# Four-layer attention kernel on one core: layer 0's slots placed anew, split weight products and split context made once, layer 2 in two blocks

## What is computed

```
# layer 0: grouped attention, 32 heads, 8 key heads, 16 wide, norm behind it
q = x@Wq+bq;  k = ctx@Wk+bk;  v = ctx@Wv+bv
x = norm(softmax(q k^T/4 + mask) v @ Wo + bo + x) * gamma + beta
# layer 1: token mixing with a state, then channel mixing
xa = norm(x);  sx = shift(xa) - xa;  t = tanh((xa + sx*maa_x) @ maa_w1)
xw, xk, xv, xr, xg = xa + sx*(maa_j + (t @ maa_w2)_j);  w = exp(-exp(...))
out_l = r_l (faaaa*k_l v_l + s);  s = k_l v_l + w_l s         # 100 steps, 32 heads
x = x + (headnorm(out) * silu(xg@Wg.T)) @ Wo.T
xc = norm(x);  x = x + sigmoid(xr2@fWr.T) * (relu(xk2@fWk.T)^2 @ fWv.T)
# layer 2: one head, 512 wide
x = x + alpha * (softmax((x w_q^T)(ctx w_k^T)^T / sqrt(512)) (ctx w_v^T)) w_o^T
# layer 3: two cross attentions (16 heads, 128 wide, one more key and value), then an MLP (2048)
x = x + attention(norm(x), ctx)   # twice;   x = x + gelu(norm(x)@w_fc1+b)@w_fc2+b
```

## Time and profile before

| | before |
|---|---|
| median of 3 runs | 2740.22 us (2735.76 to 2745.87) |
| the profiled execution's own time | 2739.51 us |
| its span, first to last instruction | 2737.7 us |
| mean granted clock of TensorE | 0.95 |
| PE busy | 2478.0 us (91%) |
| PE weight loads (PEld) busy | 2167.3 us (79%) |
| DVE busy | 1394.6 us (51%) |
| ACT busy | 1139.6 us (42%) |
| POOL busy | 1122.3 us (41%) |
| DMA | 390.93 MB, mean 143 GB/s |

### The profile page before, as it was taken

One profiled execution on the slowest core, in us unless ns is written; L12 is line 12 of the kernel. 1 busy time (PEld: TensorE's weight loads), 2 busy tenths in 40 slices (PEclk: granted clock), 3 DMA queues, 4 the chain that ended last, 5 costly groups with the idle time before them and its releaser, 6 DMA issues. The chain is left out here.

```text
span 2737.7 us, 37676 instructions
## 1 busy us (share of the span) xinstructions
PE 2478.0 (91%) x13944; PEld 2167.3 (79%) x13944; DVE 1394.6 (51%) x2335; ACT 1139.6 (42%) x2439; POOL 1122.3 (41%) x498
## 2 busy tenths in 40 slices
PE   7888679989998888899889999989997999999698
PEld 5666334479895555699889999979996999999698
DVE  4566541278885431243346666533334666665633
ACT  3677111232233211223366666622235666665321
POOL 1100322251222110452287978826215887976300
PEclk9999869999998889999999999999999999999799
DMA  7453611589993015244744544315285444442300
GB/s 227 122 122 78 213 63 48 154 245 237 235 227 125 8 54 174 90 157 165 250 152 163 161 146 156 127 53 206 103 272 178 155 138 155 145 159 85 109 29 25
DMA packets 218058, 390.93 MB, mean 143 GB/s; under 512 B 88900, under 2 KB 127836, under 8 KB 217108
## 3 DMA queue, kind: packets, MB, share of 16 engines
q1 hardware_dynamic: 217876, 388.52, 45.8%
HBM read 291.70 MB, written 104.92 MB: 145 GB/s over the span
## 5 line engine op out<-in xcount | busy, mean ns | idle before, releaser
L1851 PE MATMUL att_ring<-ca_pp,att_arena 128*128 128x400 f32 (+1 forms) x2304 | 437.5, 348 | 26.5 <-POOL att_arena L1933 14.8
L1851 PEld LDWEIGHTS att_ring<-ca_pp,att_arena 128*128 128x128 f32 (+1 forms) x2304 | 422.0, 191 | 36.0 <-POOL att_arena L1933 20.2
L1922 POOL TENSOR_TENSOR att_arena<-att_arena 128x1448 fp32r<-128x1448 f32 x64 | 212.1, 3314 | 253.6 <-ACT att_arena L1939 253.6
L1851 PE MATMUL att_ring<-att_arena,qk_wh 128*128 128x362 f32 x1024 | 255.6, 331 | 0.0
L2535 DVE TENSOR_TENSOR ca_yl<-att_ring,att_arena 128x400 fp32r<-128x400 f32 x256 | 146.6, 573 | 203.8 <-ACT att_arena L2494 203.8
L1933 POOL TENSOR_TENSOR att_arena<-state_X,att_arena 128x1536 fp32r<-128x1536 f32 x64 | 224.4, 3506 | 5.0
L1930 POOL TENSOR_TENSOR att_arena<-state_X,att_nothing 128x1536 fp32r<-128x1536 f32 x64 | 176.0, 2750 | 47.7 <-DMA state_X<-in_ctx 47.7
L1851 PE MATMUL att_ring<-att_arena,qk_wl 128*128 128x362 f32 x512 | 172.9, 338 | 18.6 <-POOL att_arena L2116 18.2
L1851 PEld LDWEIGHTS att_ring<-att_arena,qk_wh 128*128 128x128 f32 x1024 | 185.2, 192 | 0.0
L2494 ACT ACTIVATE att_arena<-att_ring 128x400 fp32r<-128x400 f32 x256 | 128.9, 503 | 92.9 <-PE att_ring L1851 92.6
L1945 ACT ACTIVATE att_kstage<-att_score,att_shift 100x362 f32<-100x362 f32 x256 | 143.8, 563 | 44.6 <-DVE att_shift L1958 44.6
(11 more groups left out here) (404 smaller groups left out, 6010.3 us busy)
## 6 DMA issues: line engine op xcount, KB each, us to landing
att_arena<-keys SPq DMA_DIRECT2D x64, 724.0 KB, 5.1
state_X<-in_ctx SPq DMA_DIRECT2D x64, 512.0 KB, 3.9
queries<-att_arena SPq DMA_DIRECT2D x16, 1600.0 KB
att_arena<-queries SPq DMA_DIRECT2D x64, 400.0 KB, 3.9
keys<-rec_stage SPq DMA_DIRECT2D x32, 724.0 KB, 4.5
keys<-att_kstage SPq DMA_DIRECT2D x32, 724.0 KB, 3.2
l_arena<-kept_value SPq DMA_DIRECT2D x176, 100.0 KB, 5.4
state_X<-in_ctx SPq DMA_DIRECT2D x64, 210.0 KB, 4.2
```

What stands on the lines that cost most here:

```text
L1851: issued = nc.tensor.matmul(out, x, y, start=(first and k == 0), stop=(last and k == count - 1))
L1922: self.nc.gpsimd.tensor_tensor(self.kl[:, n % 2].bitcast(F32R), self.kl[:, n % 2], self.kh[:, n % 2].bitcast(F32), ALU.subtract).then_inc( ...
```

## The change

1. **Layer 0's slots.** KEY_AT is 1, VALUE_AT 13 with two of twelve value matmuls a slot for six slots, AV_AT 19, the second quad at slot 6 (AV_LATE) of the next batch. The left-over rows of quad 0 go to slot 0 of the next batch, those of quad 1 to slot 9. VectorE finishes quad 0 at slot 2 and quad 1 at slot 11 of the next batch, and both quads of the last batch behind the loop. SP stores quad 0, stacks the next keys, stores quad 1; it asks for the context of batch b+2 once `value_full` has reached b+2, one more than before. The clearing of the spare piece is dropped.
2. **Weight products.** `WeightProduct` keeps a high part (ScalarE) and a low part (VectorE) and stores both. value_out is made whole in l1d, from weights loaded into rooms that are free there; its halves in l1f and l2x go. All engines wait for its stores before l1o.
3. **The norm of layer 0** also makes the row statistics for layer 1, row by row.
4. **The copies for the fill** are issued behind layer 1's ten loads and two weights more, before the norm l1a.
5. **Context parts.** A new class splits the context into high and low part once, in head_norm, l1z, l1g, l1h and l1i: ScalarE rounds, POOL subtracts, SP stores to DRAM. Layer 3 loads both parts; POOL's split there is gone.
6. **Layer 2 in two blocks**: transposes, split rows and query product in split parts; then the attention loop, with the output product and the addition inside it. The context is asked for in the first block.
7. Five semaphores of the gate's block become one.

```diff
-    KEY_AT, VALUE_AT, AV_AT = 10, 15, 20
+    KEY_AT, AV_LATE, VALUE_AT, AV_AT = 1, 6, 13, 19
...
+                    store_output(b - 1, 0)
+                if b + 1 < B:
+                    stack_keys(b + 1)
+                if b:
                     store_output(b - 1, 1)
                     pack_sums(b - 1)
-                if b + 1 < B:
-                    stack_keys(b + 1)
                 if b + 2 < B:
-                    sp.wait_ge(value_full, b + 1)
+                    sp.wait_ge(value_full, b + 2)
                     load_context(b + 2)
                 if b:
                     widen_inverse(b - 1)
-                store_output(b, 0)
+            store_output(B - 1, 0)
...
-                    if i == VALUE_AT + 4:
+                    if i == VALUE_AT + 7:
                         keep_value(b + 1)
-                if n < total and i == AV_AT + 4:
-                    finish(b, 0)
-                if n < total and b and i == AV_AT + 4 - 13:
+                if n < total and b and i == 2:
+                    finish(b - 1, 0)
+                if n < total and b and i == AV_LATE + 3 * PIECES + 2:
                     finish(b - 1, 1)
                 if n < total and b and i == TILES - 2:
                     invert_sums(b - 1)
-            normalise(B - 1, 1)
+            for quad in range(QUADS):
+                normalise(B - 1, quad)
...
-                    if VALUE_AT <= i < VALUE_AT + 3:
-                        make_values(b + 1, i - VALUE_AT)
-                if n < total and AV_AT <= i < AV_AT + 3:
+                    if VALUE_AT <= i < VALUE_AT + 6:
+                        for k in range(2):
+                            make_values(b + 1, 2 * (i - VALUE_AT) + k)
+                if n < total and AV_AT <= i < AV_AT + 3 * PIECES:
                     attend(b, 0, i - AV_AT)
-                    if i == AV_AT + 2:
-                        attend_left(b, 0)
-                past = i - (AV_AT - 13)
-                if b and 0 <= past < 3:
-                    attend(b - 1, 1, past)
-                    if past == 2:
-                        attend_left(b - 1, 1)
+                if b and i == 0:
+                    attend_left(b - 1, 0)
+                if b and AV_LATE <= i < AV_LATE + 3 * PIECES:
+                    attend(b - 1, 1, i - AV_LATE)
+                if b and i == AV_LATE + 3 * PIECES:
+                    attend_left(b - 1, 1)
...
+    def keep_high(self, act):
+        for n in range(CC):
+            act.wait_ge(self.full, n + 1)
+            self.nc.scalar.activation(self.high[:, n, :], self.banks[n][:], ACT.Copy).then_inc(self.high_kept, 1)
+
+    def keep_low(self, dve, n):
+        dve.wait_ge(self.high_kept, n + 1)
+        self.nc.vector.tensor_tensor(self.low[:, n, :], self.banks[n][:], self.high[:, n, :].bitcast(F32),
+                                     ALU.subtract).then_inc(self.low_kept, 1)
+
+    def store(self, sp, parts, stored):
+        for n in range(CC):
+            sp.wait_ge(self.low_kept, n + 1)
+            sp.dma_start(parts[:, 0, n, :], self.high[:, n, :].bitcast(F32)).then_inc(stored, 16)
+            sp.dma_start(parts[:, 1, n, :], self.low[:, n, :].bitcast(F32)).then_inc(stored, 16)
...
+                        dve.wait_ge(moved, b)
+                        nc.vector.bn_stats(next_stats[:, b - 1, :], X[:, b - 1, :])
+                    if b in (4, 6):
+                        product.keep_low(dve, b // 2 - 2)
...
-        copy_for_fill(nc, a)
...
+            start_copies(nc, weights_in, [(weight_room(key), by_chunks(a["L2_w_v"])), (weight_room(value), by_chunks(a["L2_w_oT"]))])
+            copy_for_fill(nc, a)
+            layer_norm_transposed(nc, "l1a", X, 1e-5, col("ln1_w"), col("ln1_b"), ident, lambda b: (cur[:, b],), "plain", row_stats)
             await_copies(nc, (loaded, 10))
             low, lowg, lowd = st.sb("low", [P, B, L]), st.sb("lowg", [32, B, L]), st.sb("lowd", [64, B, L])
-            shifted_difference(nc, "l1d", cur, before[:, 1], diff, [(col("maa_x"), mix[0])])
+            shifted_difference(nc, "l1d", cur, before[:, 1], diff, [(col("maa_x"), mix[0])],
+                               (weight_room(key), weight_room(value), weight_room(decay).bitcast(F32R), weight_room(mix[1]).bitcast(F32R),
+                                weights_in, 2), a["value_out"], parts_stored)
...
+            await_copies(nc, (parts_stored, 2 * CC))
             mix_and_product(nc, "l1o", mixing(0, mix[1]))
...
+    def load(self, sp, b):
+        if b >= 4:
+            sp.wait_ge(self.low_done, 3 * (b - 1))
+        sp.dma_start(self.raw_of(b)[:, 0:2], self.ctx[b, 0:2 * P, :].rearrange("(t p) c -> p t c", p=P)).then_inc(self.raw_in[b % 2], 16)
+        sp.dma_start(self.raw_of(b)[0:self.row, 2], self.ctx[b, 2 * P:S, :]).then_inc(self.raw_in[b % 2], 16)
+
+    def round(self, act, b):
+        act.wait_ge(self.raw_in[b % 2], 32 * (b // 2 + 1))
+        if b >= 2:
+            act.wait_ge(self.kept[b % 2], 64 * (b // 2))
+        self.nc.scalar.activation(self.high[b % 2][:, 0:2], self.raw_of(b)[:, 0:2], ACT.Copy).then_inc(self.high_done, 1)
+        self.nc.scalar.activation(self.high[b % 2][0:self.row, 2], self.raw_of(b)[0:self.row, 2], ACT.Copy).then_inc(self.high_done, 1)
+
+    def subtract(self, pool, b, t):
+        rows = self.row if t == 2 else P
+        pool.wait_ge(self.high_done, 2 * (b + 1))
+        self.nc.gpsimd.tensor_tensor(self.low[b % 2][0:rows, t], self.raw_of(b)[0:rows, t], self.high[b % 2][0:rows, t].bitcast(F32),
+                                     ALU.subtract).then_inc(self.low_done, 1)
+
+    def store(self, sp, b):
+        sp.wait_ge(self.low_done, 3 * (b + 1))
+        for k, part in enumerate((self.high, self.low)):
+            sp.dma_start(self.out[b, :, k, 0:2], part[b % 2][:, 0:2].bitcast(F32)).then_inc(self.kept[b % 2], 16)
+            sp.dma_start(self.out[b, 0:self.row, k, 2], part[b % 2][0:self.row, 2].bitcast(F32)).then_inc(self.kept[b % 2], 16)
...
+            head_norm(nc, y, dev, sq, means, compact, widen, col("gn_w"), col("gn_b"), gate, 1e-5, z, parts, passing((0, 1), (0,)))
+            product_rows(nc, "l1z", W["WoT"], z, add_and_sum(X, stats, added), parts=parts, batches=(1, 2), moves=passing((2, 3, 4), (1, 2)))
...
+                for n in range(CC):
+                    sp.dma_start(query_key[:, :, :, n * P:(n + 1) * P].bitcast(F32), a["query_key"][:, :, :, n * P:(n + 1) * P]).then_inc(
+                        query_key_in[n], 16)
+                load_context(sp, 0)
+                sp.dma_start(value_out[:].bitcast(F32), a["value_out"]).then_inc(value_out_in, 16)
+                sp.dma_start(alpha[:], a["alpha_rows"]).then_inc(alpha_in, 16)
+                for b in range(1, CB):
+                    load_context(sp, b)
...
+                for u, (half, n) in enumerate(slots):
+                    if half == 0:
+                        pe.wait_ge(query_key_in[n], 16)
+                    if n == 0:
+                        pe.wait_ge(rows_low, 4 * (half + 1))
+                    if u >= RB:
+                        pe.wait_ge((kept_act, kept_dve)[u % 2], (u - RB) // 2 + 1)
+                    part = slice(n * P, (n + 1) * P)
+                    products(nc, banks[u % RB][:, :, 0:L], [
+                        ((query_key[:, 0, c, part], query_key[:, 1, c, part]),
+                         (rows[:, 0, 4 * half:4 * half + 4, c, :], rows[:, 1, 4 * half:4 * half + 4, c, :])) for c in range(CC)]).then_inc(full, 1)
...
+                def output(b):
+                    pe.wait_ge(mixed_low, b + 1)
+                    if b == 0:
+                        pe.wait_ge(value_out_in, 16)
+                    if b >= 2:
+                        pe.wait_ge(added, b - 1)
+                    products(nc, outs[b % 2][0:L, :], [((rows[:, 0, b, c, :], rows[:, 1, b, c, :]), (value_out[:, 0, c, :], value_out[:, 1, c, :]))
+                                                       for c in range(CC)]).then_inc(out_full, 1)
...
                 scores(0)
                 for b in range(B):
                     if b + 1 < B:
                         scores(b + 1)
+                    if b >= 2:
+                        output(b - 2)
                     if b >= 1:
                         mix(b - 1)
                     turn_over(b)
+                output(B - 2)
                 mix(B - 1)
+                output(B - 1)
...
     def load_context(self, sp, n):
-        sp.wait_ge(self.x_ready, n)
-        b = n % B
-        sp.dma_start(self.craw[:, 0:2, :], self.ctx[b, 0:2 * P, :].rearrange("(t p) c -> p t c", p=P)).then_inc(self.x_in, 16)
-        sp.dma_start(self.craw[0:STILES[2][1], 2, :], self.ctx[b, 2 * P:S, :]).then_inc(self.x_in, 16)
+        if n >= 2:
+            sp.wait_ge(self.y_full, CC * (n - 1))
+        b, rows = n % B, STILES[2][1]
+        sp.dma_start(self.x[:, n % 2, :, 0:2].bitcast(F32), self.ctx_parts[b, :, :, 0:2]).then_inc(self.x_in[n % 2], 16)
```

(36 more changed lines are left out.)

371 lines of the change are left out of this document (192 added, 179 removed).

## The result

The changed kernel took 2731.86 us (median of 14 runs, 2727.16 to 2737.42) beside 2740.41 us for the kernel before (14 runs): the ratio is 0.9968, with a 95% interval of 0.9959 to 0.9978. I had forecast 2719 us, 21 us less. It is faster by 0.3%, 8.5 us, though inside my range. The profiled execution's span is 2728.7 us against 2737.7.

What follows compares the result with a forecast made beforehand. TensorE (PE), busy 91% of the span, was taken as the bound, its waits as the gain. Terms -26 +46 +7 +2 -4 -24 -22 = -21 gave 2718.5, said as 2719 us; range 2684 to 2752.

Steps and rivals of the forecast that it cites:

- up to 5.0 us x 6 = 30 us go: Layer 0's loop: batches 1 to 6 fall from 29.2 us towards PE's 24.2; taken as -26, bounds -10 and -30.
- Rival 3: Layer 0: context asked for later lands slowly, PE waits before the keys, 36 us, 2755; 0.10 together with other losses.
- The hold's +38: Layer 1's start: SP, held issuing fill copies, is free at about 382, so the norm starts then, not at 344.07.
- The product's +10: Layer 1's difference stage: a whole product of 32 matmuls (17.0 us) plus about 1 us replaces 7.7 us of VectorE.
- The clock's -2: Layer 1's first small product: PE is already at its upper clock when it comes, -2 us.
- Rival 1: Layer 0 to 1: SP isn't held by the fill copies; +26 instead of +46, 2699 us; chance 0.24.
- Rival 2: Layer 0 to 1: hold lasts until the last fill copy lands, 18 us more; layer 0 wins 6 less; 2743; chance 0.10.
- +7, +2 and -4: Layer 1's end: head norm's root waits for context and rounding, +7; other parts' work, +2; difference stage loses half product, -4.
- rival 4: Layer 1's end: POOL's part subtractions and VectorE slow each other over SBUF, low parts come late; 2742 us; chance 0.06.
- Layer 2: -24 forecast: Layer 2: first part 43.7 to 27 us (-17), second part -7; together -24, bounds -12 and -32.
- Layer 3: -22 forecast: Layer 3's attention blocks: PE's waits for POOL's split context and keys go, 21 us, clock 1 more; bounds -10 and -26.
- 50 GB/s more leaves room: Layer 3: doubled context loads fit, as the stage moves 139 GB/s with the DMA engines 0.43 busy.

Runs made afterwards that it cites:

- run 3: Changed kernel with SP asking for the context of batch b+2 once the values of batch b, not b+1, are made: 2731.80 us, ratio 0.9975.
- run 9: Changed kernel with nine of layer 0's transfers a batch (inverted row sums' spreading) issued by POOL instead of SP: 2723.13 us, ratio 0.9940.
- run 2: Kernel before with only the five fill copies moved behind layer 1's ten loads, ahead of the norm l1a: 2766.76 us, ratio 1.0100.
- run 1: Changed kernel with the five fill copies back ahead of layer 0's output product: 2703.69 us, ratio 0.9869.
- run 6: Changed kernel with the fill copies reordered, the four weights first and the context last: 2718.84 us, ratio 0.9930.
- run 8: Changed kernel with the first two loads of the context's parts issued ahead of the four weights at layer 1's end: 2724.63 us, ratio 0.9952.
- run 4: Changed kernel with layer 3's first context parts asked for behind the sixth store of queries, not the second, in both projections: 2720.71 us, ratio 0.9932.

## Why the prediction was wrong, by its steps

**Layer 0: -14.3 instead of -26.** The step that failed is "up to 5.0 us x 6 = 30 us go": 13.9 went. PE's work of a batch was summed well (24.2 against a measured 24.8), and the bounds named ScalarE as what could take the gain back. The bound was SP. I never summed its list of a batch, which the change leaves as long as it was: 27.5 us, hidden while PE's batches took 29.2 and above them once PE could do 24.8. Rival 3 had the place of the loss (the keys, for the context, with the clock lower behind the wait) but the wrong cause, a slow landing and a late release; run 3 took the late release away and won nothing, run 9 shortened the list and took batches 1 to 6 from 161.2 to 150.4 us, 10.8 of the 12.4 lost. Of the smaller terms, batch 0 was to gain nothing and gained 3.2 us, and the tail was to cost 2 and cost 2.9. And part of the 30 was never there to be won: the 29.2 us a batch come from one execution, 28.5 in run 2's trace.

**Layer 0 to 1: +46 forecast, +47.1 measured** (1.0 + 4.0 + 34.2 + 10.3 - 2.4). The hold's +38 counted from before the norm of layer 0 and came as 4.0 + 34.2 = 38.2; from the first of layer 1's loads to a free SP I had 41 us (382 - 341), measured are 368.3 - 328.1 = 40.2. The product's +10 was 10.3. The clock's -2 agrees with the -2.4 of its row by luck: the first small product, where I had put it, took 14.3 us instead of 13.8 at a granted clock of 0.88 instead of 0.89, and the 2.4 us lie in the last product before the recurrence and in the recurrence itself. Rival 1 (no hold) is ruled out by the 24.77 us row, and by runs 1 and 2 from both sides. The rule of the Trainium skill (DMA: Bandwidth & Descriptors, section "Issuing engines are not separate DMA queues"), that issuing is usually small beside the transfer, holds here for a load by itself (0.34 us) and not for one behind a full queue. Rival 2's clause, that the hold could last to the end of the last copy, is ruled out too: run 6 freed SP with most of the copies still to go. My own measure, SP free once the context copy is through, fits the changed kernel (SP free at 368.3, the copy landed at 369.1) but isn't the rule either, as run 6 had the whole copy still to go.

**Layer 1's end: +7, +2 and -4 forecast, +8.1 and -6.8 measured.** The head norm was right, and run 8 shows its cause. The -6.8 are some -5 of the difference stage with the norm ahead of it and -2 of the four products with parts, for which I had +2. So the parts' work cost nothing that shows, and rival 4 (POOL and VectorE in turn, as the Trainium skill's page "SBUF — State Buffer", section "SBUF: two separate sides", would have it) is out as a price. The turn itself is there, in both kernels. In the kernel before, in the last product of layer 1, VectorE's addition of two SBUF tiles took 1.48 us where a subtraction of POOL had begun 0.11 us before it, and 0.69 where POOL stood still:

```profile
988.55 1.05 POOL L1613 TENSOR_TENSOR l1i_sl<-l_arena,l1i_sh 128x400 fp32r<-128x400 f32 x1 [2.63 <-ACT l1i_sh L1635]
```

```profile
988.66 1.48 DVE L1503 TENSOR_TENSOR state_X<-state_X,l1e_tmp 100x512 f32<-100x512 f32 x1
...
1002.69 0.69 DVE L1503 TENSOR_TENSOR state_X<-state_X,l1e_tmp 100x512 f32<-100x512 f32 x1
```

With a subtraction of the parts beside it the same addition took up to 1.90 us in the changed kernel. It reached nothing: behind it VectorE still stood waiting for PE's next product.

**Layer 2: -24 forecast, -29.7 measured**, inside the bounds. The first part is 24.6 us for 27, with hardly any of the 3 us of waiting that I added for rows of 512 bytes; the second 70.6 for 74.

**Layer 3: -22 forecast, -13.2 measured.** The attention blocks gave more than I said (-27.5 from first to last matmul, with the clock at 1.00). What failed is "50 GB/s more leaves room". It was read from the attention block, where the stage moves 139 GB/s, and there it held (193 GB/s now); but the first load of parts is issued in the projection, with the weights for the values and the queries right behind it, in a stretch that already moved 288 GB/s. The projections, for which I had no term, took 14 us more. Of these run 4 shows 8 to be the load's place ahead of those weights; the other 6 are open. The change also moved this load past a wait, but that did nothing: SP reached it 163.4 us behind the projection's first matmul, and 163.5 in the kernel before. What is left of the change there is the doubled size, which no run takes back by itself.

In sum: layer 0 and layer 3 came out 11.7 and 8.8 us worse than forecast, the others together 8 us better.

## What to carry to other kernels

Before you spread PE's slots, sum the list of every engine that issues or waits in the loop, the DMA issuer's own waits included: the longest list is the next bound, and an earlier release doesn't help a transfer that stands late in it. Treat a bulk copy as an instruction of the engine that issues it, and put it where a long block covers the hold, for the barrier behind it handed the hold to all engines here. When a load grows, look at the DMA traffic of the stretch in which it is issued, not of the one that uses it.

## What the runs showed of the hardware

SP is held in an issue when its queue has no room, and the room goes by packets rather than by bytes or transfers. I counted it in the records of packets, as those issued but not yet started. In the changed kernel SP issued nine loads of layer 1 in 0.3 to 0.6 us each; the tenth took 1.29 us and left some 2,000 packets (4 MB) pending, and the next took 3.19. When SP came free of the fill copies, 1,956 packets (4.0 MB) had still to start in the changed kernel, and 1,851 (3.8 MB) in run 2; in run 6, where the context's 128 packets of 46 KB went last, it was 1,725 packets but 9.2 MB. So long rows at the end of a series free the issuer early (352.9 against 368.3 us). The room itself I can only bracket: issues that had been held ended with between some 1,500 and 2,000 packets pending.

VectorE and POOL take turns where VectorE adds two SBUF tiles and POOL subtracts two: 1.48 us instead of 0.69 for the addition, which ended 0.54 us after POOL's subtraction, in the rows above.
